# Taking 1012 spare bf16 products off TensorE in an eight-stage layer kernel

## What is computed

```python
x = x + delta_rule(layernorm(x), ...)      # 16 heads of 8: state += clip(0.9 k (v - k.state)); out = clip(state q)
x = x + ffn0(layernorm(x), ...)            # shared SwiGLU plus top-2 of 8 experts
x = x + palette(layernorm(x), ...)         # top-15 earlier tokens, small MLP on each, bilinear look-up in a 16x16 palette
x = x + ffn0(layernorm(x), ...)
x = x + linear_attention(layernorm(x), ...)  # elu+1 features, 16 heads, causal
x = x + ffn1(layernorm(x), ...)            # 8 experts in bf16, top-2, plus a shared one
x = x + decay_attention(layernorm(x), ...)
x = x + ffn1(layernorm(x), ...)
```

## Time and profile before

| | |
|---|---|
| time, median of 3 runs | 1498.96 us (1495.59 to 1512.79) |
| span of the profiled execution | 1705.2 us |
| TensorE (PE) busy in it | 84% |
| VectorE (DVE) busy | 61% |
| ScalarE (ACT) busy | 49% |
| GpSimd (POOL) busy | 51% |
| mean granted clock of TensorE | 0.867 of 2.4 GHz |

### The profile page before, as it was taken

One profiled execution on the slowest core, in us unless ns is written; L12 is line 12 of the kernel. 1 busy time (PEld: TensorE's weight loads), 2 busy tenths in 40 slices (PEclk: granted clock), 3 DMA queues, 4 the chain that ended last, 5 costly groups with the idle time before them and its releaser, 6 DMA issues.

```text
span 1705.2 us, 54458 instructions
## 1 busy us (share of the span) xinstructions
PE 1432.7 (84%) x22044; PEld 939.2 (55%) x22044; DVE 1046.2 (61%) x4618; ACT 836.0 (49%) x2249; POOL 877.8 (51%) x1399
## 2 busy tenths in 40 slices
PE   2687878988979897998988889798997979888987
PEld 1243445555656464655656565575755556656664
DVE  2877656775656575576656757567774765464442
ACT  1232333464554454555545555456472545545655
POOL 2447456565636455465455547456554546545331
PEclk8679889987878898898779989788997979798999
DMA  5000010000000000000000000100000010100000
GB/s 151 2 1 26 8 28 17 17 15 18 9 23 5 22 9 15 18 8 20 11 24 8 15 19 6 28 3 23 10 6 25 6 27 10 27 14 20 3 5 6
DMA packets 24294, 30.12 MB, mean 18 GB/s; under 512 B 9089, under 2 KB 18978, under 8 KB 24034
## 3 DMA queue, kind: packets, MB, share of 16 engines
q0 software_dynamic: 8304, 16.73, 3.8%
q1 hardware_dynamic: 15730, 9.82, 2.0%
HBM read 25.21 MB, written 2.29 MB: 16 GB/s over the span
## 4 chain that ended last, share of the span: by engine, by line
PE 64%; DVE 12%; issue 9%; ACT 7%; POOL 3%; another core or an unknown queue 3%; SPq 1%; DMA 0%; DVEq 0%; ACTq 0%; POOLq 0%
PE ps L521 11%; PE ps L757 4%; PE ps L745 3%; PE ps L663 3%; PE ps L715 3%; PE ps L561 3%; PE ps L737 2%; DVE ps L961 2%; PE ps L575 2%; PE ps L585 2%; PE ps L861 2%; PE ps L602 2%; PE ps L853 2%; PE ps L688 2%
## 5 line engine op out<-in xcount | busy, mean ns | idle before, releaser
L521 PE MATMUL ps<-sb 128*128 128x512 bf16 x1012 | 318.7, 423 | 5.4 <-issue 1.2
L961 DVE TENSOR_TENSOR_SCAN ps<-ps,sb 128x47 f32<-128x47 f32 (+3 forms) x1024 | 271.0, 265 | 44.0 <-DVE ps L953 1.0
L1781 POOL DMA_INDIRECT sb<-table,sb x240 | 234.2, 976 | 121.3 <-issue 61.1
L953 DVE TENSOR_TENSOR ps<-sb,ps 128x24 f32<-128x24 f32 (+3 forms) x1024 | 192.3, 188 | 14.8
L1649 POOL TENSOR_TENSOR sb<-sb 128x1 f32<-128x1 f32 x128 | 72.7, 568 | 222.0 <-DVE sb L896 221.4
L521 PEld LDWEIGHTS ps<-sb 128*128 128x128 bf16 x1012 | 95.7, 106 | 95.2 <-issue 38.8
L969 DVE TENSOR_TENSOR sb<-ps,sb 128x32 f32<-128x32 f32 x254 | 46.0, 181 | 119.7 <-PE ps L575 87.4
L745 PE MATMUL ps<-sb 15*32 15x16 f32 x4096 | 69.7, 190 | 48.8 <-issue 48.7
L976 DVE TENSOR_TENSOR ps<-sb,ps 128x12 f32<-128x12 f32 x254 | 40.9, 161 | 107.4 <-PE ps L585 88.6
L585 PEld LDWEIGHTS ps<-sb 32*32 32x32 f32 x2032 | 43.6, 109 | 113.3 <-issue 83.4
L1297 ACT ACTIVATE sb<-sb 128x128 f32<-128x128 f32 x128 | 62.3, 489 | 71.4 <-POOL sb L1651 71.1
(11 more groups left out here) (309 smaller groups left out, 3765.0 us busy)
## 6 DMA issues: line engine op xcount, KB each, us to landing
sb<-table,sb POOLq DMA_INDIRECT x240
sb<-in_cs SPq DMA_DIRECT2D x16, 128.0 KB
table<-sb SPq DMA_DIRECT2D x17, 64.0 KB, 1.5
sb<-in_x SPq DMA_DIRECT2D x4, 256.0 KB, 9.5
sb<-dscr SPq DMA_DIRECT2D x64, 2.0 KB
out<-sb SPq DMA_DIRECT2D x16, 64.0 KB, 1.5
sb<-in_mdn POOLq DMA_DIRECT2D x1, 512.0 KB, 9.3
sb<-in_wex SPq DMA_DIRECT2D x1, 512.0 KB, 6.5
```

The costliest lines, as they stand in the source:

```text
L521: e.matmul(b[:, 0:512], identb[:, :], mup[:, 0:512], start=True, stop=True)
L953: e.tensor_tensor(at(psP, p + ROW - 3 - 2 * m, [ROW, 3], [2, m], [1, 2]), AC[:, row(n, k), :, HIST - 2 * m:HIST].rearrange("p r (a b) -> p ...
L961: e.tensor_tensor_scan(at(psD, 16 + k + COMB * skip, [COMB, 3 * ROW - skip]), at(psP, p + skip, [1, 3 * ROW - skip]), Q[:, i % 32, skip:3 ...
L1781: e.indirect_dma_start(GA[:, k, :], None, table[0:128 * i + 128, :] if i else table0, bass.IndirectOffsetOnAxis(u[:, k:k + 1], 0)).then_in ...
```

## The change

`FILL`, the counter `idle`, the function `fill`, the hook `before` of `fast` and the spare products in `bank` are taken out. With them goes the wait for the bf16 constants in front of a spare product; stages that use these constants wait for them themselves. All other instructions, their order, their other waits and the rotation of the banks stay.

```diff
-    def fast(engine, stages, before=lambda n: None):
+    def fast(engine, stages):
...
-        for n, letter in enumerate(ORDER[engine]):
-            before(n)
+        for letter in ORDER[engine]:
             next(runs[letter])
...
-        idle = [0]
 
         def bank(key, *until):
 
             b, old = bk.take(key, *until)
             for sem, val in old:
                 w.wait_ge(sem, val)
-            if idle[0]:
-                w.wait_ge(*loaded("bf"))
-            for _ in range(idle[0]):
-                e.matmul(b[:, 0:512], identb[:, :], mup[:, 0:512], start=True, stop=True)
-            idle[0] = 0
             return b
-
-        def fill(n):
-            idle[0] = int(FILL[n])
...
-        fast("PE", stages, fill)
+        fast("PE", stages)
```

More of the change, by code:

```diff
@@ L199 @@
 }
[L200 to L220, removed]
```

## The result

The changed kernel takes 1544.69 us (median of 4 runs, 1534.24 to 1556.10) against 1500.22 us for the kernel before on the same chip: the ratio is 1.029, with a 95% interval of 1.021 to 1.037. It is slower by about 44 us. The forecast was 1534 us and +2.3%.

The account below looks back on a forecast made before the run. TensorE was taken as the bound, busy 84% of the span and carrying 64% of it on the chain. -92 us given back and +132 us of clock made +40 us of 1705.2, or 1534 us; own range 1514 to 1604.

Parts of the forecast that it names:

- The time given back, -92 us: Spare products out of TensorE's list: half of their 184 us on the chain comes off the span, between 0 and 184.
- the 184 us of the chain: Spare products' share of the critical chain: 10.8% of the 1705.2 us profiled span, the most that could be given back.
- Two places, one of each kind: At line 853, 0.215 us per spare product comes back; elsewhere 2.97 us of idle time follows and nothing comes back.
- The clock, 0.867 to 0.72: TensorE's mean clock without spare products, set just under the 0.74 of the first 100 us; ends 0.80 and 0.60.
- What the clock costs, +132 us: TensorE's wide real products grow by 163 us at clock 0.72, 0.81 of it on the chain; between +54 and +288.
- 800 us of wide products: TensorE's real work that stretches with the clock, after 314 us of issue-bound narrow products are taken as untouched.
- The 1114 us of real work: TensorE's busy time of 1432.7 us less the spare products' 318.7 us.
- The sum, +40 us: Whole kernel: -92 + 132 us of 1705.2, or +2.3%, carried to the timed 1498.96 us as 1534 us.
- the two cancel: Rival: a gain of 120 to 140 us against the +132, time within 1% of 1499 us; chance 0.15.
- mostly load: Rival: the full 184 us comes back against the same 132, giving -52 us, -3.0%, or 1453 us; chance 0.21.
- the clock holds: Rival: real work alone keeps TensorE's clock near 0.867, only -92 us remain, 1418 us; chance 0.06.
- The rival by the skill's page: Clock ramp under 1% of the span: clock term under 17 us, sum about -75 us; no separate chance given.

Follow-up runs that it names:

- the narrow products: Kernel before with its 1012 spare products on a 32x32 corner, all 512 columns kept: 1.108 and 1.096 of the kernel before on slow chips, 1.147 on a quick one.
- e7_narrow2: Kernel before with its 1012 spare products on a 32x32 corner of the array, slow chip: ratio 1.096 to the kernel before.
- e4_after: The changed kernel, no spare products, against the kernel before on a slow chip: 1718.84 us against 1712.87, ratio 1.001.

## Why the prediction came out right

**That the change trades two terms.** Right, and the narrow products took the two apart. Without the narrow products this would have stayed an argument, since before and after differ in both at once.

**The time given back, -92 us: half of the 184 us of the chain.** Two places, one of each kind, stood behind the half, so that it is near is in part luck. What was measured is more, 159 us on the slow chip and some 177 us on the quick one. But these are the amounts for spare products at the low clock, where a 512-column one lasts 582 ns in the median instead of the 379 of the earlier trace rows, so they overstate what the change itself gave back. The row of the narrow kernel (run e7_narrow2; least, median, largest ns):

```profile
L521 PE MATMUL ps<-sb x1012: 371/582/629, 45.8 to 1865.8; 32*32 32x512 bf16 x169
```

An estimate for the clock of before: of the 165 us between narrow and full, the part that goes with the spare products' own 73 of 225 us is 53 us. That leaves 159 - 53 = 106 us given back on the slow kind, 58% of the 184. No run measured it by itself.

**The clock, 0.867 to 0.72.** On the slow kind of chip, from which 0.867 came, it fell to 0.757, between the 0.72 taken and the end of 0.80; on the quick kind from 0.932 to 0.807. The fall was 0.11 to 0.13 and not 0.147. Reading it from the stretch with fewest spare products gave about the size, from a stretch with other stages in it.

**What the clock costs, +132 us.** By the same estimate, 165 - 53 = 112 us on the slow kind: the term was too large, and its factors erred against each other. First, the fall was taken too deep, to 0.72. Second, the rule that 800 us of wide products grow by the ratio of the mean clocks gives too little: 125 us for a fall from 0.867 to 0.750, where from full to narrow products the real work grew by 152 us. Work is not spread evenly over fast and slow time, and the prediction named this as one side of the error. Third, 0.81 of the real work was put on the chain; 165 us of time for 225 us of busy time is 0.73.

The 1114 us of real work was itself a low reading, since the subtraction drops what overlaps with spare products. In the changed kernel on a slow chip (e4_after) nothing overlaps with them, and TensorE's head has 1337.1 us at a clock of 0.757, against 1266.5 us in the narrow kernel at 0.750:

```profile
PE 1337.1 (78%) x21032; PEld 938.2 (55%) x21032; DVE 1046.9 (61%) x4618; ACT 836.0 (49%) x2249; POOL 876.7 (51%) x1399
```

So some 71 us between 1114 and 1337 are overlap come to light and not growth. Merged, the intervals of the real products cover 1204 us in the trace of before and 1337 in this one.

**The sum, +40 us.** On the quick chip it was +44 us. But the sum was made on a trace of the slow kind and carried over as a percentage, and on that kind the same change costs +6 us of 1713 (1.001, interval 0.997 to 1.006). There the sum was off by 34 us, by the estimate 14 in the time given back (106 for 92) and 20 in the clock (112 for 132). The step "1705.2 us stands to 1499 us as 1 to 0.879" is the one that failed, and the forecast came out near by luck: on quick chips the clock is worth 5.1 points more than on slow ones (14.7 against 9.6) and the load 2.3 points more (11.8 against 9.5), and this happened to bring back what the sum had too much for the slow kind. The span was 14% off the timed runs, and that was a sign of another chip with other proportions, to be looked into before anything was carried over. The rival "the two cancel" is what happens on slow chips; "mostly load" and "the clock holds" are out on both kinds.

**The rival by the skill's page.** The Trainium skill, in "TensorE: Matmul & The Clock Gate", the part on the HAM clock gate, puts the ramp at under 1% of a span. Taken as the whole cost of the lower clock, as the prediction took it, the runs disagree: 39% of the time at the lower level after, and 9.6 to 14.7 points between narrow and full spare products. The same part says that activity lifts the clock. On slow chips the clock is 0.757 without spare products, 0.87 with full ones and 0.750 with narrow ones, so the trace agrees for full products alone.

**What would show it.** Four signs were named. The chain with TensorE first at over 53%: 56% on both kinds. The clock from 0.68 to 0.78: 0.757 on the slow kind, but 0.807 on the quick, where 0.80 or above was to mean at most half of the clock term; the quick chip started from 0.932, so the fall, not the level, was what to name. Real work over 1200 us: 1253, but this could not tell, since the merged real work is 1204 us with the spare products still in. TensorE's waits for VectorE and ScalarE hardly growing would have meant that the time given back was the larger term; the three largest went from 49 to 107 us, though some growth had to come once no spare product stood in these waits.

## What to carry to other kernels

Work that only keeps TensorE's clock up is worth having where TensorE would wait, and is load where the next product is ready: count the two from the waits of a trace without it. On slow chips that paid (0.985); on quick ones, where the clock was worth more, nothing tried was shown to beat all 1012. To size the clock's worth, keep the load and take the array's work away (same columns, a corner of the array); the difference is the clock's, with its share for the spare products themselves. Do not subtract one group's busy time from an engine's whole where neighbours overlap; compare two kernels with the same overlaps, or merge the intervals of the rest. When a profiled span is far from the timed runs, find out first whether it is from the same chip.

## What the runs showed of the hardware

- On slow chips the clock was 0.740 to 0.750 with 1012 spare products on a 32x32 corner of the array with all their 512 columns, 0.757 with none, and 0.87 with 1012 on the full array.
- The first 1012 full products go with a rise of the clock from 0.757 to 0.87, the next 1012 with one to 0.899. In between, 314 and 698, in other places, have 0.799 and 0.836.
- A 512-column spare product lasts at least 371 ns on the 32x32 corner and 376 ns on the full array: the same time for a sixteenth of the array.
- The kernel before takes 1500 us on some chips and 1712 us on others, with the same busy time of VectorE (1049 and 1046 us), a clock of 0.93 against 0.87, and 21.5 against 105 us of pauses before the narrow products of three lines. The change was worth 3% on one kind and nothing shown on the other.
